# A two-layer graph kernel: TensorE sums two supertiles of layer 0 in every second step, VectorE selects before it picks

## The reference, cut to what matters

```python
h = jnp.maximum(_layernorm(x, axis=-1), 0.0)              # x: 12500 nodes x 32 features
x = x + segment_sum(h[src] * edge_weight[:, None], dst)   # layer 0: 400000 edges, dst sorted
h = jnp.maximum(_layernorm(x, axis=-1), 0.0)
x = x + _L1_gnn_ref(h, ...)                               # layer 1: messages through a small MLP
```

## Time and profile before

| | |
|---|---|
| median of the runs | 6549.67 us (6548.87 to 6551.32) |
| the profiled execution | 6552.7 us |
| its span, first to last instruction | 6550.9 us |
| mean granted TensorE clock | 0.986 of full speed |
| busy, share of the span | TensorE 93%, VectorE 87%, GpSimd 73%, ScalarE 44% |
| picks (L705), TensorE | 2628.7 us busy, 12180 matmuls |
| gathers (L464), GpSimd | 4708.7 us busy, 4964 gathers in both layers |
| pick tables (L1018), VectorE | 916.5 us busy, 870 tables |

### The profile page before, as it was taken

One profiled execution on the slowest core, in us unless ns is written; L12 is line 12 of the kernel. 1 busy time (PEld: TensorE's weight loads), 2 busy tenths in 40 slices (PEclk: granted clock), 3 DMA queues, 4 the chain that ended last, 5 costly groups with the idle time before them and its releaser, 6 DMA issues.

```text
span 6550.9 us, 157240 instructions
## 1 busy us (share of the span) xinstructions
PE 6086.5 (93%) x42909; PEld 4939.4 (75%) x42909; DVE 5711.8 (87%) x13211; ACT 2879.8 (44%) x12179; POOL 4752.8 (73%) x5071
## 2 busy tenths in 40 slices
PE   5999999999999999998899999999999999999998
PEld 4888888888888888886677777777777777777775
DVE  7777777777777777777899999999999999999997
ACT  2222222222222222223655565556556556555665
POOL 4777777777777777776777777777777777777776
PEclk9999999999999999998999999999999999999998
DMA  4111111111111111111211111111111111111111
GB/s 104 32 30 32 30 32 30 32 31 32 30 33 30 32 30 32 31 32 26 51 39 38 40 39 38 38 40 38 39 39 37 40 39 37 39 37 41 39 37 35
DMA packets 293178, 243.20 MB, mean 37 GB/s; under 512 B 106611, under 2 KB 289619, under 8 KB 292679
## 3 DMA queue, kind: packets, MB, share of 16 engines
q0 software_dynamic: 158848, 81.65, 9.4%
q1 hardware_dynamic: 133500, 158.02, 8.5%
q10 hardware_dynamic: 802, 3.22, 0.2%
HBM read 237.26 MB, written 5.25 MB: 37 GB/s over the span
## 4 chain that ended last, share of the span: by engine, by line
PE 45%; DVE 33%; issue 15%; DVEq 4%; POOL 1%; DMA 1%; ACT 0%; POOLq 0%; SPq 0%; ACTq 0%
PE w_ps L705 31%; PE hp_ps L855 5%; DVE prod L1186 5%; DVE p L1171 3%; DVE pick L1018 3%; PE w_ps L785 3%; DVE t L1202 3%; DVE z L1237 3%; DVE prod L1178 3%; DVE reduced_sb L1148 2%; DVE prod L1031 2%; DVE z L1035 2%; DVE vsh L1164 1%; DVE reduced_sb L1147 1%; PE w_ps L715 1%
## 5 line engine op out<-in xcount | busy, mean ns | idle before, releaser
L464 POOL DMA_INDIRECT z<-h_table,idx x4964 | 4708.7, 949 | 1721.5 <-issue 1504.4
L705 PE MATMUL w_ps<-parts,pick 128*128 128x448 f32 x12180 | 2628.7, 371 | 205.0 <-DVE z L1035 140.2
L705 PEld LDWEIGHTS w_ps<-parts,pick 128*128 128x128 f32 x12180 | 2250.2, 188 | 419.3 <-issue 123.1
L566 ACT ACTIVATE z<-z,squares 128x32 f32<-128x32 f32 x3132 | 772.1, 309 | 2228.3 <-DVE z L1035 2215.6
L855 PE MATMUL hp_ps<-parts,pick 128*128 128x448 f32 x6020 | 1341.2, 373 | 43.5 <-DVE squares L1230 42.3
L855 PEld LDWEIGHTS hp_ps<-parts,pick 128*128 128x128 f32 x6020 | 1096.6, 188 | 281.4 <-DVE squares L1230 138.0
L785 PE MATMUL w_ps<-w_sb,squares 64*128 64x256 f32 x6264 | 1073.6, 386 | 0.2 <-ACT squares L617 0.2
L785 PEld LDWEIGHTS w_ps<-w_sb,squares 64*128 64x128 f32 x6264 | 912.7, 193 | 54.2 <-ACT squares L617 0.7
L1018 DVE TENSOR_TENSOR pick<-sc_ps,feat 128x896 fp32r<-128x896 f32 x870 | 916.5, 1087 | 40.0 <-issue 36.4
L1178 DVE TENSOR_TENSOR prod<-w_ps,squares 128x384 f32<-128x384 f32 (+1 forms) x1044 | 778.9, 746 | 1.3 <-ACT squares L623 1.3
L620 ACT ACTIVATE scalars<-z 128x48 f32<-128x48 f32 x522 | 151.0, 289 | 1307.1 <-DMA z<-h_table,idx 1307.1
(11 more groups left out here) (91 smaller groups left out, 4709.3 us busy)
## 6 DMA issues: line engine op xcount, KB each, us to landing
z<-h_table,idx POOLq DMA_INDIRECT x4964, 2.4
squares<-in_ft_sh SPq DMA_DIRECT2D x261, 216.0 KB, 2.5
feat<-key_table SPq DMA_DIRECT2D x260, 192.0 KB, 3.0
feat<-key_table SPq DMA_DIRECT2D x260, 128.0 KB
h_table<-big SPq DMA_DIRECT2D x10, 280.0 KB
rel_sb<-in_dst_t SPq DMA_DIRECT2D x1, 1566.0 KB, 8.2
idx_all<-in_src_t SPq DMA_DIRECT2D x1, 1530.0 KB, 10.6
squares<-in_ew_t SPq DMA_DIRECT2D x1, 1530.0 KB, 14.1
```

The costliest lines, as they stand in the source:

```text
L464: pool.indirect_dma_start(z[:, r, u, :], None, rows, bass.IndirectOffsetOnAxis(ap=idx[:, r, u:u + 1], axis=0)).then_inc(z_in[r], 16)
L566: last = nc.scalar.activation(z[:, r, u, :], z[:, r, u, :], ACT.Copy, scale=ew_all[:, bass.ds(n * G + u, 1)])
L705: mm = pe.matmul(fold_ps[:, pick_banks[k], 0:NC * D], pick[:, k, blk, :], parts[:, t, :, blk, :], start=(blk == 0 and t == 0), stop=(blk = ...
```

## The change

In layer 0, TensorE makes no sum in even steps. In an odd step n it makes two, those of n - 5 and n - 4, one after the other, behind the picks of n; one wait, that n - 6 is in `acc`, stands before both. VectorE's step n now has `onehot` and selections of n - 3 first, then the pick tables of n + 1, and then the addition of n - 6 (before: n - 5). In its step 0 it builds the tables of 0 as well. VectorE gets 6 steps more than supertiles and writes out its last ring of six instead of looping over it. Numbers of matmuls, gathers, pick tables, selections and additions stay as they are.

```diff
-                if s is None or s >= 4:
-                    v = (r - 4) % R0
-                    pe.wait_ge(msg0_ready, n - 3)
-                    if s is None or s >= 6:
+                if r % 2 and (s is None or s >= 5):
+                    if s is None or s >= 7:
                         pe.wait_ge(acc0_done, n - 5)
-                    for u in range(G):
-                        mm = pe.matmul(total0_ps[v % 2], z[:, v, u, :], onehot[:, v, u, :],
-                                       start=(u == 0), stop=(u == G - 1))
-                    mm.then_inc(sum0_ready, 1)
+                    for late in (5, 4):
+                        v = (r - late) % R0
+                        pe.wait_ge(msg0_ready, n - late + 1)
+                        for u in range(G):
+                            mm = pe.matmul(total0_ps[v % 2], z[:, v, u, :], onehot[:, v, u, :],
+                                           start=(u == 0), stop=(u == G - 1))
+                        mm.then_inc(sum0_ready, 1)
...
-                if s is None or s < S:
+                if s == 0:
                     make_picks(b, r, s)
...
-                if s is None or s >= 5:
-                    if s == 5:
+                if s is None or s + 1 < S:
+                    make_picks(*before(b, r, R0, -1), None if s is None else s + 1)
+                if s is None or s >= 6:
+                    if s == 6:
                         dve.wait_ge(cleared, 2)
-                    base = first_column(n - 5)
-                    dve.wait_ge(sum0_ready, n - 4)
-                    take_sums(n - 5, None if s is None else s - 5, base, acc0_done, total0_ps[(r - 5) % 2])
+                    base = first_column(n - 6)
+                    dve.wait_ge(sum0_ready, n - 5)
+                    take_sums(n - 6, None if s is None else s - 6, base, acc0_done, total0_ps[r % 2])
...
-            supertiles(dve, R0, layer0, lag=5)
+            supertiles(dve, R0, layer0, lag=6, written_out=1)
```

## The result

The changed kernel takes 6384.22 us (median of four runs, 6382.98 to 6385.23) against 6550.18 for the kernel before on the same chip: a ratio of 0.9747, interval 0.973 to 0.9763. That is 166 us less; 6380 was forecast, between 6368 and 6446. The profiled execution took 6384.63 us, its span is 6382.8. Lines of the code stand one or a few further down: picks stay at L705, sums are at L716, the addition at L1009, `onehot` at L997, the pick tables at L1019, the selection ends at L1036. In the experiments, lines are counted as in the kernel that each one edits, or up to four further down.

A forecast was written before the change was run, and what follows sets the result against it. TensorE and VectorE waiting on each other set today's pace; GpSimd was to become the bound. Gathers -163.2, end -6.8, start 0 make -170 us: profiled 6552.7 to 6382.7, median 3 below, 6380 us; range 6368 to 6446.

The forecast's parts named there:

- TensorE's part: TensorE's picks and sums in layer 0: 16.40 us per period without waits, 15.95 with sums paired, each pair saving 0.30.
- The rival in which a pair saves nothing: TensorE stays the bound at 16.40 us per period against 17.21: -139 us, 6411 us; chance 0.11.
- VectorE's part: VectorE's work per supertile is only moved, none added; 14.2 us per period, below TensorE's 15.95.
- (a): VectorE's selections come first, some 2.0 us before TensorE's next pick; the 0.98 us wait goes, with 0.9 to spare.
- (b) to (d): Tables one step ahead in free slots; VectorE meets pair ends only in even steps; TensorE's wait for n - 6 is met.
- The rival of a wait that comes back: Picks wait 0.84 us after every pair because the first selection is late; nothing gained, 6550 us; chance 0.04.
- GpSimd's part: GpSimd's gathers never lack work and become the bound: 26 need 32.53 us against TensorE's 31.90 per six steps.
- the rival in which it starves on the paired release: GpSimd without backlog idles 2.5 us in each six steps, 87 times: +54 us, 6604 us; chance 0.04.
- The gaps of 2.7 us: GpSimd's 23 gaps, one every 91 gathers, 2.42 us too long each, go with waiting and vanish; if they stay, 56 us.
- The rival does not fit either: Rival that GpSimd's gaps belong to layer 0's loop and stay: 6380 + 56 = 6436 us; chance 0.24.
- The sum: Layer 0 total: 2227 gather steps -163.2 us, end after the last gather -6.8, start 0 within 4; together -170 us.
- The clock: Rival that waits at pairs lower TensorE's clock, 2.4 us less 0.2 at each of 261 pairs: +570, 6950 us; chance 0.01.

The follow-up runs named there:

- the three operations put in: Changed kernel with three more VectorE operations of a pick table's size ahead of `onehot`, in one step of six behind a pair: 6489.15 us, ratio 0.9903.
- the new order alone: Kernel before with only VectorE's selections first and tables one supertile ahead; TensorE still makes one sum per step: 6409.6 us, ratio 0.979.
- run 2227: No run number: 2227 counts gather steps; that run is the changed kernel with one more VectorE operation in one step of six, 6382.28 us.

## Why the prediction was right, point by point

**TensorE's part** held in both sizes: 16.40 us per period without pairs (16.41 found) and 15.95 with them (15.96), each in a kernel where TensorE was busy 1000 of 1000 us. The rival in which a pair saves nothing falls with it.

**VectorE's part.** (a) The wait of 0.98 goes, with room to spare: 0.9 us was worked out, 1.0 found. The working behind it was a little off. I had the selection 2.0 us behind the end of the pair, and it comes 1.64 us behind (1527.29 against 1525.65), because VectorE's addition needs the first of the two sums alone. (b) to (d) show no cost: no pick waits for a table in the loop, and TensorE waits for no addition. The rival of a wait that comes back is told from the forecast by the three operations put in: it takes more than 1.0 us of delay.

**GpSimd's part** held: it is the bound, and 13 gathers take 2786.2 / 2227 x 13 = 16.26 us, as forecast. Behind the first gather of the sum no idle time of it is over 0.32 us, so the rival in which it starves on the paired release does not happen. The Trainium skill (GPSIMD Engine Reference, Specifications) states more narrowly than the prediction has it that the interfaces shared with VectorE are contended where a VectorE instruction has two SBUF inputs or runs in a 2-port mode. No run here shows a slowing: VectorE went from 759 to 791 us busy, and a gather takes 946 ns before and after the earlier trace rows.

**The gaps of 2.7 us** did go, and the 56 us with them, so the forecast came out. Half of the reason that I gave is borne out: where GpSimd is always behind there are none. In the profiles of the changed kernel, of its repeat, of it with one more gather and of it with one more VectorE operation, no idle time of GpSimd behind the first gather of the sum is over 0.32 us. The other half, that they go with waiting, is not. The kernel before with one more gather and the changed kernel with fewer gathers wait for sums as well, and their longest issue waits between 1000 and 2000 us are 0.4 and 0.3 us, where the kernel before has 2.72. To that extent the term came out by luck. The rival does not fit either: the gaps are not a fixed cost of layer 0's loop. With the new order alone they are still there, but at most 1.6 us long between 1000 and 2000 us, some 1.2 too much; seven periods of 91 gathers in that kernel leave GpSimd 7 x (16.41 - 13 x 1.249) = 1.2 us. A fixed gap of 2.42 would have made GpSimd the bound in that kernel, at 16.23 + 2.42 / 7 = 16.58 us per period; TensorE's 16.41 stood.

**The sum.** Gathers: -163.2 forecast, -163.0 found. Start: 0 within 4, found -1.3. End: -6.8 forecast, -4.6 found. This is the one term that was mis-sized: the last gather took 4.74 us from issue to ScalarE's start, where I had put 2.4 for its landing, and the last sum 0.85 instead of 0.57 us. Together the span came out 2 us longer than forecast (0.2 + 2.2 - 1.3, and 0.9 in the rest of the program). The other 2 us to the median are not of the kernel's mechanism: I put the median 3 us below the profiled execution, as it was before, and here it lies 0.4 below.

**The clock** is 1.00 in the loop in every kernel shown above. In the kernel before, behind the idle 5.31 us, it was 0.50 from 105 to 108 us, which is 1.2 GHz. The waits of up to 0.5 us at the pairs did not bring that level, nor did those of 1.67 us in the run with three operations. What the Trainium skill states on bursts (TensorE: Matmul & The Clock Gate, HAM oscillation), that a wait in every round can bring the low clock back in every round, no run here shows in the loop.

What is left: GpSimd's 32.53 us and TensorE's 31.91 per six steps are now 2% apart. What follows is an estimate from these numbers. Giving one gather of every ring to TensorE would cost it a pick of 2.86 us for 1.25 saved, which makes it 34.8 us, slower than either. Only a share of the rings, about one in seven ((32.53 - 31.91) / (1.25 + 2.86) = 0.15), would balance the two, and gain 0.19 us per ring, 16 us in all. That was not tried, since the loops go over rings that are all alike.

## What to carry to other kernels

An engine whose busy share is 76% can be full, and one at 71% was 5% from it: add the issue time that precedes each of its instructions, take the rate from a stretch in which it has work waiting, and put that floor beside the bound's before adding up gains. Two repairs of one wait do not add: each alone gave 140 us, both 166 to 175, as the next engine stood 5% below. To find out who bounds, give the suspect one more instruction and one less, in the kernel before as well: 0 and 0 there, +99 and -48 us here.

## What had not been expected

**Where the gaps end.** In the kernel before, each of the 23 gaps of GpSimd ends within 0.01 us of the start of a sum of TensorE, though the profile names nothing that it waited for. GpSimd's timeline (the earlier trace rows have the gather after the gap, at 1550.15) and TensorE's around one:

```profile
1546.48 0.95 POOL L464 DMA_INDIRECT z<-h_table,idx  x1 [0.30 <-issue]
```

```profile
1546.60 0.56 PE L715 MATMUL w_ps<-onehot,z 128*32 128x32 f32 x12
...
1550.15 0.57 PE L715 MATMUL hp_ps<-onehot,z 128*32 128x32 f32 x12
```

The gap goes from 1547.43 to 1550.15, and the next sum starts at 1550.15. The loop repeats itself, so the 23 are closer to one observation than to 23. With the new order alone the gaps end at the start of a sum as well, but other runs do not make it a rule. In the kernel before with fewer gathers, and in the new order with fewer, they are 1.86 us long, come once per 96 gathers (four rings of 24), and end where a sum ends. GpSimd's and TensorE's timelines of the former:

```profile
1738.92 0.94 POOL L464 DMA_INDIRECT z<-h_table,idx  x1 [1.86 <-issue]
```

```profile
1738.36 0.56 PE L716 MATMUL w_ps<-onehot,z 128*32 128x32 f32 x12
```

With the three VectorE operations they are 1.0 us long, come once per 182 gathers (seven rings), and end 3.55 us behind the start of a sum. So neither the length, nor the count, nor the place is fixed, and the cause stays open: the runs changed the number of gathers and the order of VectorE, and none singles it out.

**Two paces of a gather.** Gathers take 946 ns in some profiles and 944 in others, with the same work on GpSimd. The changed kernel and its repeat have 946. The changed kernel with one more VectorE operation, GpSimd alone from 112 to 2890 us:

```profile
L464 POOL DMA_INDIRECT z<-h_table,idx x2225 | 2099.9, 944 | 678.1 <-issue 668.4 <-PE w_ps L716 6.4 <-PE hp_ps L716 3.4
```

In that run 2227 steps of a gather take 2780.6 us (110.77 to 2891.32), in the changed kernel's profiled run 2786.2. The 5.6 us are the distance between that kernel's run of 6377, the one profiled, and its others of 6382 to 6384. The repeat of the changed kernel has the same distance within its four runs, 6377 to 6378 three times and 6383.47 once; only the run of 6383.47 was profiled, so that a gather takes 944 ns in the others is likely but not shown. What sets the pace of a run is not known.
